# Values by four column tiles, and two mixes side by side, in the first of two window-attention blocks

## The chip, the cores and the metric

The kernel runs on one core of a Trainium2 chip. The metric is the time of one execution on the device in microseconds (us), the median of several. The core's engines are TensorE (PE, with its weight loads shown as PEld), VectorE (DVE), ScalarE (ACT), GpSimd (POOL) and SyncE (SP), which issues the transfers. Each engine works through its own list of instructions in order; semaphores tie the lists together.

## What is computed

Two transformer blocks over 32 images of 56 x 56 tokens with 96 features, float32 in and out. The first has 12 heads and windows of 7 x 7 tokens, shifted by three. The second has 6 heads and windows of 8 x 8. Of the first, cut:

```
xw = windows of roll(x, (-3, -3))                    # 2048 windows of 49 tokens, 96 features
q, k, v = split(xw @ qkv_w + qkv_b)                  # 12 heads of 8 features
attn = cosine(q, k) / max(tau, 0.01) + bias + mask
out = softmax(attn) @ v                              # per window and head
x = x + layernorm(roll back(out @ proj_w + proj_b))
x = x + layernorm(gelu(x @ fc1_w + fc1_b) @ fc2_w + fc2_b)
```

## The kernel before

The first block (`swin_block`) takes its 2048 windows in 256 groups of eight: four pairs of two windows, 392 tokens. The second (`plain_block`) follows when the first is done; the change doesn't touch it.

Each engine has a function `body(g, phase)` that lists its work for one step, written out by hand, and `run_groups` runs it for every group, in a loop over 56 steps written out. The groups are staggered: in step `g`, TensorE turns the input of group `g + 2` and makes its keys, queries and values, scores the pairs of group `g`, turns and mixes the exponentials of group `g - 1`, projects group `g - 2`, and does the MLP of groups `g - 3` and `g - 4`. In a call the first argument is that offset. So `mix(-1, 2)` is the mix of pair 2 of the group before. The order of these calls in `body` is the order in which TensorE works.

TensorE's stages that matter here, with their lines:

- `keys` and `queries` (products at L445 to L447): three products each, stationary 96 x 96, 392 moving columns. `hidden` uses the same lines for its three chunks.
- `turn_probs` (L480): three transposes of a pair's exponentials. ScalarE copies them to `probT` (L623).
- `mix` (L494): exponentials times values for the two windows of a pair. The output's features stand on partitions 0 to 95 in three bands of 32, so each matmul has 32 stationary columns and takes one of three column tiles: 12 matmuls, 24 records, since a float32 matmul shows as two. For pairs 1 and 3 the sums of the exponentials follow (L498), 6 matmuls in the same tiles.
- `values` (L522): for each of eight windows and for the even and the odd heads, one matmul with the window's 49 tokens as stationary columns and 48 moving columns of the weights. Even heads go to PSUM partitions 0 to 48, odd ones to 64 to 112: 16 matmuls, 32 records. ScalarE spreads them to `v_heads` (L663).
- `scores` (L470): stationary 32 x 64, 12 matmuls a pair.
- `key_norms` (L538), `query_norms` (L543): one product each over squared keys and queries.

Three banks of PSUM, A, B and C, serve all dense products by turns. `free(...)` ahead of a stage makes TensorE wait until the bank's last reader is done: the queries' bank by the GELU of the hidden layer's second chunk (`hid`, L700), the query norms' bank by the spreading of the values (`v_heads`, L663). ScalarE does the exponentials, the copies of `probT`, the GELUs with two loads of function tables around them, and several more; VectorE the scores' bias and maxima, the readings of keys and queries and the residuals.

Of the kernel before, what the change touches and what calls it, by code (L numbers as in the profile page):

```python
# [42 lines left out]
HALF = 64  # L43
# [70 lines left out]
def before(group, slot, lag):  # L114

    while slot < lag:
        group, slot = group - 1, slot + PAIRS
    return group, slot - lag


def exists(group, groups):
    return not isinstance(group, int) or 0 <= group < groups
# [14 lines left out]
def swin_block(nc, cfg, src, dst, par, const, psum):  # L137
    win, heads, groups = (cfg.win, cfg.heads, cfg.groups)
    WIN = win * win
    NT = WINDOWS * WIN  # L140
    NTP = NT + 16
    D = DIM // heads
    J = 32 // D
    HP = heads // 2
# [7 lines left out]
    with ctx:  # L152

        def sb(name, shape, dtype=F32):
            return ctx.enter_context(nc.sbuf_tensor(f'{cfg.name}_{name}', shape, dtype))
        did = {name: ctx.enter_context(nc.semaphore(f'{cfg.name}_{name}')) for name in STEPS}

        def upto(group, index=0, per=1):
            return count_for(group, index, per, groups)
        psS = psum['scores']  # L160
        psP = psum['probs']
        psM = psum['dense']
# [30 lines left out]
        xT = sb('xT', [128, 2, NT])  # L193
# [195 lines left out]
        with nc.Block() as block:  # L389
# [47 lines left out]
            def _(pe):  # L437

                def body(g, phase):

                    def parity(d):
                        return (phase + d) % 2
# [6 lines left out]
                    def all_windows(first):  # L449
                        part, pair, column = [list(d) for d in first.ap]  # L450
                        return bass.AP(first.tensor, first.offset, [part, pair, [HALF, 2], column])

                    def free(*uses):
                        for name, d, *place in uses:
                            if exists(g + d, groups):
                                pe.wait_ge(did[name], upto(g + d, *place))
                                break
# [15 lines left out]
                    def turn_probs(d, p, part):  # L473
                        if exists(g + d, groups):
                            pe.wait_ge(did['prob'], upto(g + d, p, PAIRS))
                            ug, us = before(g + d, p, 1)
                            pe.wait_ge(did['probT'], upto(g + d, 2 * p, 2 * PAIRS) if part else upto(ug, 2 * us + 1, 2 * PAIRS))
                            for n in range(3):
                                hp = 3 * part + n
                                last = nc.tensor.transpose(psP[:, n * QT:(n + 1) * QT], prob[0:QT, p, 2 * hp:2 * hp + 2, :].rearrange('p h k -> p (h k)'), ident[0:QT, 0:QT])  # L480
                            last.then_inc(did['prob_turned'], 1)

                    def mix(d, p):
                        if exists(g + d, groups):
                            pe.wait_ge(did['v_heads'], upto(g + d))
                            pe.wait_ge(did['probT'], upto(g + d, 2 * p + 1, 2 * PAIRS))
                            if p % 2 == 0:
                                mg, ms = before(g + d, p, 2)
                                pe.wait_ge(did['mixedT'], upto(mg, ms // 2, 2))
                            for half in range(2):  # L490
                                first = p % 2 * TT + half * WIN
                                for n in range(HB):
                                    for band in range(BANDS):
                                        last = nc.tensor.matmul(psO[32 * band:32 * band + 32, first:first + WIN], v_heads[:, (phase + d) % 4, 2 * p + half, band, n, :], probT[:, p, band * HB + n, half * HALF:half * HALF + WIN], start=n == 0, stop=n == HB - 1)  # L494
                            if p % 2 == 1:
                                for n in range(HB):
                                    for band in range(BANDS):
                                        last = nc.tensor.matmul(psO[32 * band:32 * band + 32, SUMS:SUMS + 2 * TT], sum_heads[:, n, :], all_windows(probT[:, p - 1:p + 1, band * HB + n, 0:WIN]), start=n == 0, stop=n == HB - 1)  # L498
                            last.then_inc(did['mixed_made'], 1)
# [15 lines left out]
                    def values(d, bank):  # L515
                        if exists(g + d, groups):
                            pe.wait_ge(did['xT'], upto(g + d))
                            for w in range(WINDOWS):
                                for odd in range(2):
                                    cols = w_qkv[:, 2 * DIM:3 * DIM].rearrange('c (h o d) -> c h o d', o=2, d=D)[:, :, odd, :]  # L520
                                    out = psM[odd * HALF:odd * HALF + WIN, bank, w * HP * D:(w + 1) * HP * D]
                                    last = nc.tensor.matmul(out, xT[:, parity(d), w * WIN:(w + 1) * WIN], cols, start=True, stop=True)  # L522
                            last.then_inc(did['v_made'], 1)

                    def keys(d, bank):
                        if exists(g + d, groups):
                            pe.wait_ge(did['xT_low'], upto(g + d))
                            product(psM[0:DIM, bank, 0:NT], w_qk_high[:, DIM:2 * DIM], w_qk_low[:, DIM:2 * DIM], xT_high[:, parity(d), :], xT_low[:, parity(d), :]).then_inc(did['k_made'], 1)

                    def queries(d, bank):  # L530
                        if exists(g + d, groups):
                            pe.wait_ge(did['xT_low'], upto(g + d))
                            product(psM[0:DIM, bank, 0:NT], w_qk_high[:, 0:DIM], w_qk_low[:, 0:DIM], xT_high[:, parity(d), :], xT_low[:, parity(d), :]).then_inc(did['q_made'], 1)
# [58 lines left out]
                    turn_probs(-1, 3, 1)  # L592
                    free(('hid', -3, 0, CHUNKS), ('proj_read', -2), ('sq_norm', 1), ('k_read', 1))
                    keys(2, C)
                    mix(-1, 2)
                    free(('hid', -3, 1, CHUNKS), ('x1T_low', -3), ('xT', 2), ('q_read', 1))
                    queries(2, A)
                    turn_probs(0, 0, 0)
                    mix(-1, 3)
                    free(('hid', -3, 2, CHUNKS), ('fc2_read', -4), ('sq_norm', 1), ('v_heads', 1))  # L600
                    values(2, B)
                    scores(0, 3)
                    turn_probs(0, 0, 1)
                    free(('k_read', 2), ('hid', -3, 0, CHUNKS), ('proj_read', -2), ('sq_norm', 1))
                    key_norms(2, C)
                run_groups(pe, groups, 56, body, 16)

            @block.scalar
# [1085 lines left out]
```

## Time and profile before

| | us |
|---|---|
| median of 3 timed runs | 7237.07 (7237.04 to 7237.53) |
| the profiled execution, its time | 7242.55 |
| its span, first to last instruction | 7240.7 |
| TensorE matmuls busy | 6900.7 (95%) |
| TensorE weight loads busy | 5347.6 (74%) |
| ScalarE busy | 6114.9 (84%) |
| VectorE busy | 5941.3 (82%) |
| GpSimd busy | 5286.9 (73%) |

The mean granted clock of TensorE is 0.989 of full speed over the span. The first block takes the first three fifths of it. Busy times are unions: an instruction's time runs from its start until its last result is written, and matmuls follow each other much faster than that, so a stage's cost is read from the starts in a timeline. In a timeline each line merges the neighbouring instructions of one source line: start, time from the first one's start to the last one's end, engine, line, operation, what it writes and reads, shapes (stationary, then moving) and count.

### The profile page before, as it was taken

The page shows a single profiled execution, that of the slowest core. Times are in us where ns is not written, and L with a number is a line of the kernel's source. Part 1 is how long each engine was busy: PE and PEld are TensorE (multiplying, and loading weights), DVE is VectorE, ACT ScalarE, POOL GpSimd, SP SyncE. Part 2 cuts the span into 40 slices and gives each one's busy share as a digit, 9 for nine tenths or more (in the row PEclk, how much of TensorE's full clock was granted, in tenths as well). Part 3 has the DMA queues.
Part 4 walks back from the last instruction along what each step waited for, and adds up shares of the span by engine and source line. Part 5 has one row for each costly group of instructions (what it writes and reads, how often), then busy time and mean ns, then how long its engine had stood idle before and what let it go on. Part 6 is the DMA issues. An engine that isn't in the chain of part 4 may idle for free. (4 is left out here: it accounts for less than half of the span.)

```text
span 7240.7 us, 343768 instructions
## 1 busy us (share of the span) xinstructions
PE 6900.7 (95%) x127358; PEld 5347.6 (74%) x127358; DVE 5941.3 (82%) x12726; ACT 6114.9 (84%) x11052; POOL 5286.9 (73%) x5958
## 2 busy tenths in 40 slices
PE   6999999999999999999999996999999999999998
PEld 4777777777777777777777774777777777777777
DVE  5888888888888888888888884777777777777776
ACT  5999999999999999999999995777777777777777
POOL 3777777777777777777777775777676776776775
PEclk9999999999999999999999997999999999999999
DMA  0111111111111111111111110111111111111111
GB/s 20 30 29 30 29 30 30 29 30 30 30 30 29 30 30 29 30 29 29 30 29 30 29 29 24 42 46 47 45 47 45 45 47 45 47 46 45 46 46 41
DMA packets 367729, 254.62 MB, mean 35 GB/s; under 512 B 271816, under 2 KB 347336, under 8 KB 366152
## 3 DMA queue, kind: packets, MB, share of 16 engines
q1 hardware_dynamic: 366154, 233.04, 12.5%
q8 instruction: 1060, 17.37, 1.0%
q14 instruction: 515, 4.22, 0.2%
HBM read 78.64 MB, written 77.07 MB: 22 GB/s over the span
## 5 line engine op out<-in xcount | busy, mean ns | idle before, releaser
L880 POOL TENSOR_TENSOR swin_score<-swin_score,swin_top 113x588 f32<-113x588 f32 x1024 | 1202.9, 1175 | 744.3 <-DVE swin_top L752 743.8
L623 ACT ACTIVATE swin_probT<-swin_ps_probs 128x339 f32<-128x339 f32 x2048 | 921.8, 450 | 198.5 <-PE swin_ps_probs L480 177.3
L480 PE MATMUL swin_ps_probs<-swin_ident,swin_prob 113*128 113x113 f32 x6144 | 991.1, 270 | 7.0 <-ACT swin_probT L623 7.0
L480 PEld LDWEIGHTS swin_ps_probs<-swin_ident,swin_prob 113*128 113x128 f32 x6144 | 667.4, 141 | 355.3 <-issue 321.5
L747 DVE TENSOR_TENSOR swin_score<-swin_ps_scores,swin_bias_tab 113x588 f32<-113x588 f32 x1024 | 777.1, 759 | 173.7 <-PE swin_ps_scores L470 172.4
L752 DVE TENSOR_REDUCE swin_top<-swin_score 113x12 f32<-113x588 f32 x1024 | 768.8, 751 | 0.2
L1574 POOL TENSOR_TENSOR plain_xT_high<-plain_xT,plain_one 96x512 fp32r<-96x512 f32 x196 | 203.2, 1037 | 719.0 <-ACT plain_xT L1398 719.0
L629 ACT ACTIVATE swin_prob<-swin_score 113x588 f32<-113x588 f32 x1024 | 719.1, 702 | 5.8 <-POOL swin_score L880 2.9
L783 DVE SCALAR_TENSOR_TENSOR swin_x<-swin_y,swin_y_rstd,swin_x_res 98x96 f32<-98x96 f32 x1024 | 601.2, 644 | 0.8 <-POOL swin_y_rstd L898 0.7
L494 PEld LDWEIGHTS swin_ps_mixed<-swin_probT,swin_v_heads 128*32 128x32 f32 x24576 | 422.6, 109 | 223.8 <-issue 145.8
L470 PE MATMUL swin_ps_scores<-swin_k_heads,swin_q_hat 32*64 32x196 f32 (+1 forms) x12288 | 577.7, 347 | 4.8 <-DVE swin_score L747 4.8
L563 PE MATMUL swin_ps_dense<-swin_w_fc,swin_hid 128*98 128x96 f32 x6144 | 575.2, 250 | 1.2 <-ACT swin_hid L700 1.2
L494 PE MATMUL swin_ps_mixed<-swin_probT,swin_v_heads 128*32 128x49 f32 x24576 | 563.3, 210 | 3.2 <-DVE swin_mixedT L760 1.6
L563 PEld LDWEIGHTS swin_ps_dense<-swin_w_fc,swin_hid 128*98 128x98 f32 x6144 | 556.9, 167 | 1.5 <-ACT swin_hid L700 1.5
L1305 PE MATMUL plain_ps_dense<-plain_w_fc,plain_hid 128*64 128x96 f32 x9408 | 439.9, 250 | 73.0 <-ACT plain_v_heads L1390 71.3
L1441 DVE TENSOR_REDUCE plain_top<-plain_ps_scores 128x6 f32<-128x384 f32 x784 | 427.6, 545 | 90.0 <-PE plain_ps_scores L1233 85.8
L1305 PEld LDWEIGHTS plain_ps_dense<-plain_w_fc,plain_hid 128*64 128x64 f32 x9408 | 403.9, 138 | 106.8 <-ACT plain_v_heads L1390 103.1
L886 POOL TENSOR_TENSOR swin_x_res<-swin_x_in,swin_res_row 98x384 f32<-98x384 f32 x256 | 256.2, 1001 | 291.0 <-DVE swin_x L783 235.4
L1262 PEld LDWEIGHTS plain_ps_probs<-plain_ident,plain_prob 128*128 128x128 f32 x2352 | 264.5, 142 | 271.4 <-issue 242.2
L1262 PE MATMUL plain_ps_probs<-plain_ident,plain_prob 128*128 128x128 f32 x2352 | 412.4, 285 | 54.9 <-ACT plain_probT L1363 52.1
L1369 ACT ACTIVATE plain_prob<-plain_score 128x384 f32<-128x384 f32 x784 | 388.9, 519 | 89.0 <-DVE plain_score L1443 83.5
L1375 ACT ACTIVATE plain_hid<-plain_ps_dense,plain_b_fc 128x512 f32<-128x512 f32 x588 | 404.1, 687 | 69.7 <-PE plain_ps_dense L1215 51.1
(191 smaller groups left out, 20635.4 us busy)
## 6 DMA issues: line engine op xcount, KB each, us to landing
swin_k_heads<-swin_k_hat SPq DMA_DIRECT2D x1024, 36.8 KB
plain_x_in<-between_blocks SPq DMA_DIRECT2D x784, 48.0 KB, 2.2
plain_k_heads<-plain_k_hat SPq DMA_DIRECT2D x392, 96.0 KB, 2.5
out_dram<-plain_x SPq DMA_DIRECT2D x784, 48.0 KB
swin_x_in<-in_x SPq DMA_DIRECT2D x224, 136.5 KB
between_blocks<-swin_x SPq DMA_DIRECT2D x224, 136.5 KB
swin_x_in<-in_x SPq DMA_DIRECT2D x224, 19.5 KB
between_blocks<-swin_x SPq DMA_DIRECT2D x224, 19.5 KB
```

Source lines behind the costliest of these rows:

```text
L470: last = nc.tensor.matmul(psS[half * HALF:half * HALF + rows, band, 0:BC], q_hat[part, parity(d), w * WIN:w * WIN + rows], k_heads[part, p ...
L480: last = nc.tensor.transpose(psP[:, n * QT:(n + 1) * QT], prob[0:QT, p, 2 * hp:2 * hp + 2, :].rearrange('p h k -> p (h k)'), ident[0:QT, 0 ...
L494: last = nc.tensor.matmul(psO[32 * band:32 * band + 32, first:first + WIN], v_heads[:, (phase + d) % 4, 2 * p + half, band, n, :], probT[: ...
L563: last = nc.tensor.matmul(psM[0:TT, bank, p * DIM:(p + 1) * DIM], hid[:, c, p * TT:(p + 1) * TT], w_fc2[:, c, :], start=c == 0, stop=c == ...
L623: nc.scalar.activation(to, psP[:, 0:3 * QT], ACT.Copy).then_inc(did['probT'], 1)
L629: nc.scalar.activation(prob[0:QT, p, :, 0:WIN], score[0:QT, p % 2, :].rearrange('p (h k) -> p h k', k=WIN), ACT.Exp).then_inc(did['prob'], 1)
L747: nc.vector.tensor_tensor(score[0:QT, p % 2, :].rearrange('p (b n) -> p b n', b=BANDS), psS[0:QT, :, 0:BC], kind, ALU.add).then_inc(did['s ...
L752: nc.vector.tensor_reduce(top[0:QT, p % 2, :], score[0:QT, p % 2, :].rearrange('p (h k) -> p h k', k=WIN), AX.X, ALU.max).then_inc(did['to ...
L783: last = nc.vector.scalar_tensor_tensor(x1[:, p, :], y[:, p, :], y_rstd[:, p:p + 1], x_res[:, (phase + d) % 4, p, :], ALU.mult, ALU.add)
L880: nc.gpsimd.tensor_tensor(view, view, bcast(top[0:QT, p % 2, :], 2, WIN), ALU.subtract).then_inc(did['shifted'], 1)
L1262: last = nc.tensor.transpose(psP[:, hp * QT:(hp + 1) * QT], prob[0:QT, p, 2 * hp:2 * hp + 2, :].rearrange('p h k -> p (h k)'), ident[0:QT, ...
L1305: last = nc.tensor.matmul(psM[rows:rows + HALF, bank, p * DIM:(p + 1) * DIM], hid[:, c, p * TT + rows:p * TT + rows + HALF], w_fc2[:, c, : ...
```

## The change

In the first block's `values`, each matmul is cut in two along the stationary operand: tokens 0 to 31 and tokens 32 to 48 of the window. The outputs of one window then start on PSUM partitions 0, 32, 64 and 96, which are four column tiles of 32; moving columns, order of windows and results stay. It makes 32 matmuls (64 records) of 16.

In TensorE's list, `mix(-1, 2)` moves from its place between keys and queries to behind `turn_probs(0, 0, 0)`, so that it stands right ahead of `mix(-1, 3)`, and that one right ahead of `values`, as before.

```diff
                             for w in range(WINDOWS):
                                 for odd in range(2):
                                     cols = w_qkv[:, 2 * DIM:3 * DIM].rearrange('c (h o d) -> c h o d', o=2, d=D)[:, :, odd, :]
-                                    out = psM[odd * HALF:odd * HALF + WIN, bank, w * HP * D:(w + 1) * HP * D]
-                                    last = nc.tensor.matmul(out, xT[:, parity(d), w * WIN:(w + 1) * WIN], cols, start=True, stop=True)
+                                    for a, b in ((0, 32), (32, WIN)):
+                                        out = psM[odd * HALF + a:odd * HALF + b, bank, w * HP * D:(w + 1) * HP * D]
+                                        last = nc.tensor.matmul(out, xT[:, parity(d), w * WIN + a:w * WIN + b], cols, start=True, stop=True)
                             last.then_inc(did['v_made'], 1)
...
                     turn_probs(-1, 3, 1)
                     free(('hid', -3, 0, CHUNKS), ('proj_read', -2), ('sq_norm', 1), ('k_read', 1))
                     keys(2, C)
-                    mix(-1, 2)
                     free(('hid', -3, 1, CHUNKS), ('x1T_low', -3), ('xT', 2), ('q_read', 1))
                     queries(2, A)
                     turn_probs(0, 0, 0)
+                    mix(-1, 2)
                     mix(-1, 3)
                     free(('hid', -3, 2, CHUNKS), ('fc2_read', -4), ('sq_norm', 1), ('v_heads', 1))
                     values(2, B)
```

## Rows read from the trace of the kernel before

**Rows 1.** The page's first line.
```profile
span 7240.7 us, 343768 instructions
```

**Rows 2.** Busy time of each engine (instructions), 300 to 4300 us; granted clock, DMA.
```profile
300.00:4300.00 4000.00, 3989.60 (x67137) 3027.99 (x67136) 3561.48 (x5931) 3734.89 (x7118) 3094.56 (x3321) 1.00 0.11 30
```

**Rows 3.** Waits, 300 to 4300 us: who for whom; total us, times, longest.
```profile
ACT swin_probT L623 <- PE swin_ps_probs L480: 159.4, 475, 2.4
...
PE swin_ps_dense L512 <- issue: 8.8, 3, 3.2
...
PE swin_ps_mixed L494 <- DVE swin_mixedT L760: 1.6, 1, 1.6
```

**Rows 4.** TensorE's timeline through one group, 2000 to 2018 us.
```profile
2000.30 0.82 PE L538 MATMUL swin_ps_dense<-swin_qk_sq,swin_same_head 96*96 96x392 f32 x2
...
2001.30 0.82 PE L543 MATMUL swin_ps_dense<-swin_qk_sq,swin_same_head 96*96 96x392 f32 x2
...
2009.09 0.51 PE L480 MATMUL swin_ps_probs<-swin_ident,swin_prob 113*128 113x113 f32 x3
...
2009.81 0.34 PE L447 MATMUL swin_ps_dense<-swin_x1T_high,swin_w_fc_low 96*128 96x392 f32 x1
2009.99 0.34 PE L445 MATMUL swin_ps_dense<-swin_x1T_high,swin_w_fc_high 96*128 96x392 f32 x1
...
2012.04 0.42 PE L445 MATMUL swin_ps_dense<-swin_xT_high,swin_w_qk_high 96*96 96x392 f32 x1
...
2012.75 0.55 PE L494 MATMUL swin_ps_mixed<-swin_probT,swin_v_heads 128*32 128x49 f32 x24
2013.23 0.42 PE L445 MATMUL swin_ps_dense<-swin_xT_high,swin_w_qk_high 96*96 96x392 f32 x1
...
2013.66 0.34 PE L447 MATMUL swin_ps_dense<-swin_xT_high,swin_w_qk_low 96*96 96x392 f32 x1
2013.84 0.45 PE L480 MATMUL swin_ps_probs<-swin_ident,swin_prob 113*128 113x113 f32 x3
2014.23 0.55 PE L494 MATMUL swin_ps_mixed<-swin_probT,swin_v_heads 128*32 128x49 f32 x24
2014.60 0.84 PE L498 MATMUL swin_ps_mixed<-swin_probT,swin_sum_heads 128*32 128x196 f32 x12
2015.38 0.94 PE L522 MATMUL swin_ps_dense<-swin_w_qkv,swin_xT 128*49 128x48 f32 x32
2016.24 0.56 PE L470 MATMUL swin_ps_scores<-swin_k_heads,swin_q_hat 32*64 32x196 f32 x12
...
2017.08 0.82 PE L538 MATMUL swin_ps_dense<-swin_qk_sq,swin_same_head 96*96 96x392 f32 x2
```

**Rows 5.** The same in short windows, which leave the last records of a stage.
```profile
2014.30 0.47 PE L494 MATMUL swin_ps_mixed<-swin_probT,swin_v_heads 128*32 128x49 f32 x20
...
2015.12 0.33 PE L498 MATMUL swin_ps_mixed<-swin_probT,swin_sum_heads 128*32 128x196 f32 x1
...
2015.87 0.45 PE L522 MATMUL swin_ps_dense<-swin_w_qkv,swin_xT 128*49 128x48 f32 x12
...
2016.11 0.21 PE L522 MATMUL swin_ps_dense<-swin_w_qkv,swin_xT 128*49 128x48 f32 x1
```

**Rows 6.** ScalarE's timeline in the same group; in brackets idle time before and releaser.
```profile
2009.64 0.46 ACT L623 ACTIVATE swin_probT<-swin_ps_probs 128x339 f32<-128x339 f32 x1 [0.18 <-PE swin_ps_probs L480]
...
2011.40 1.07 ACT L700 ACTIVATE swin_hid<-swin_ps_dense,swin_b_fc 128x392 f32<-128x392 f32 x2
...
2016.50 0.97 ACT L663 ACTIVATE swin_v_heads<-swin_ps_dense 49x384 f32<-49x384 f32 x2
```

**Rows 7.** TensorE's timeline in the second block, 5500 to 5516 us.
```profile
5503.69 1.03 PE L1245 MATMUL plain_ps_mixed<-plain_v_heads,plain_probT 128*32 128x34 f32 x96
5504.65 1.14 PE L1282 MATMUL plain_ps_dense<-plain_w_qkv,plain_xT 128*64 128x48 f32 x32
```

## The prediction

> **What bounds the kernel now.** I read the page first: one span of 7240.7 us [rows 1]. The kernel runs two blocks one after the other, and the change touches the first alone, so I cut a stretch out of the first block and asked for the busy time of each engine in it [rows 2]. TensorE is busy for 3989.60 of 4000 us at full granted clock (1.00, the 2.4 GHz level). ScalarE has 3734.89, VectorE 3561.48, GpSimd 3094.56. A busy TensorE in this profile is not TensorE at its peak, so the next view is the waits of the same stretch [rows 3]: there TensorE waits four times, some 10 us in all, against 159.4 us that ScalarE's copies of the turned exponentials alone wait for TensorE. So the others wait for TensorE and it waits for nobody: its instruction stream sets the time, and every 0.01 us taken out of a group of eight windows is worth 2.56 us, since the block has 256 groups.
>
> The third view is TensorE's timeline through one group [rows 4]. From one squared-norm product to the same one of the next group it is 16.78 us (2000.30 to 2017.08). In this view I read starts and not durations: an instruction's duration contains its way through the array, and the next one starts long before. What a stage costs is the distance from its start to the next stage's start. The reader is to see that these distances are larger where the shape of the stationary operand changes. One of the six-product runs (keys, queries, hidden layer) goes at 0.18 us a product when the product before it had the same shape: 2009.81 to 2009.99. The first product after a mix takes longer: the queries go from 2013.23 to 2013.66 in two steps, 0.43 us, where two even steps would be 0.36.
>
> **The change, part by part.** All of it is in three pieces, and none adds a DMA or a semaphore.
>
> *A. The mix of pair 2 leaves its place between keys and queries.* Before, keys, mix and queries take 1.80 us, from 2012.04 to the turn at 2013.84 [rows 4]. Without the mix, keys and queries are six products in a row. The first one still follows a turn and costs what it costs the queries now, 0.43 - 0.17 = 0.26 us, and the other five 0.18 us each, the last one's step to the turn included (2013.66 to 2013.84 is 0.18): 1.16 us. That is 0.64 us less. The mix now stands behind the turn and ahead of the other mix. One of the two pays the start behind a turn, as the mix at 2014.23 does today, 0.37 us up to the sums at 2014.60. The other runs on without one. Its price is that of the inner sets: the last 20 matmul records of that mix take from 2014.30 to 2014.60 [rows 5]; three column tiles work side by side, so these are 6.7 sets of three, 0.045 us each by rounded starts. With 0.37 us for all eight sets, start-up included, a set can't be over 0.046; I take 0.044, so 8 x 0.044 = 0.35 us. A = -0.64 + 0.35 = -0.29 us. Bounds: a set at 0.046 and products at 0.185 would give -0.25; a set at 0.040 gives -0.32.
>
> *B. From the sums to the values.* The sums are 12 records in four sets. They start at 2014.60 and the last starts at 2015.12 [rows 5]; with 0.015 us between the tiles of a set that is 0.167 us a set. The values start at 2015.38, 0.78 us behind the first sum, so the fourth set is followed by 0.26 us, not by 0.17. Here the shape goes from 32 columns to 49. With values by 32 columns it stays as it is between mix and sums, where no such gap stands, and I cost it at four sets, 0.67 us. B = -0.11 us. If the gap belongs to the new operands and not to the shape, B is 0.
>
> *C. The values themselves.* Now: 32 records, two tiles side by side, 16 sets, 0.86 us up to the scores at 2016.24. The last six sets go from 2015.87 to 2016.11 [rows 5], five steps and 0.01 us, 0.046 us a set; the whole from 2015.38 to 2016.11 is 15 steps and 0.01, so the first was some 0.03 us longer. From the last record to the scores it is 0.13 us. After: each product becomes two, of 32 and 17 stationary columns, so 64 records and 64 weight loads, four tiles side by side and still 16 sets, because each tile has the same eight windows with the same 48 moving columns in two records each. What is a set worth? The trace has no values by four tiles of this width, so I bound it by rows. The mix moves 49 columns with 32 stationary ones at 0.044; with 48 that is 0.043, which I take, since it is the nearest row in both sizes. Not above 0.046, which 49 stationary columns now need. Four tiles side by side do exist in this trace: the second block's mix, 96 records of 32 stationary and 34 moving columns, from 5503.69 to 5504.65 [rows 7], 0.96 us with its way out, 0.040 us for four. So C is 15 x 0.043 + 0.02 (four tiles start some 0.007 apart) + 0.13 on the way out = 0.80 us against 0.86: C = -0.06 us, with -0.11 (0.040 a set) and 0 (0.046 a set, start-up kept) as ends. The way out keeps its price, as the scores have another shape either way.
>
> **Sum.** -0.29 - 0.11 - 0.06 = -0.46 us. 256 x 0.46 = 118 us. The profiled execution has a span of 7240.7 and a time of 7242.55 us, the median of the timed ones is 7237.07; the saving comes off each of them: 7237 - 118 = 7119 us. The three bounds together give 0.25 to 0.54 us a group.
>
> **What must hold for that.** TensorE is now earlier by 0.46 us in the second half of a group, so its waits there lose as much slack. Three of them matter, all on ScalarE, whose order is fixed. First, the queries wait for the second GELU (their bank). They start at 2012.66 instead of 2013.23; the two GELUs end at 2011.40 + 1.07 = 2012.47 [rows 6], so 0.19 us are left. ScalarE itself is not earlier, its copy at 2009.64 waits for TensorE's turn at 2009.09 in the part that does not change. If the GELU were later, turn, both mixes, values and scores behind the queries in TensorE's queue would all be late with it. Second, the turn of the new group's first pair moves from 2013.84 to 2013.20 and waits for the copy behind the GELUs; that one, 0.46 us long [rows 6], ends at 2012.93 at the latest, so 0.27 us are left. Third, the query norms need the bank that ScalarE frees when it has spread the values: 2016.50 + 0.97 = 2017.47 [rows 6], and they start 1.00 us behind the key norms, at 2018.08; after the change at 2017.62. That leaves 0.15 us, the smallest margin, and it also caps the gain: the loop from TensorE's turn (2009.09) over ScalarE (2017.47) and back over TensorE (1.00 us into a group, to 8.79 us into it) is 8.38 + 7.79 = 16.17 us and a release (that copy starts 0.04 us behind the turn's end, 2009.09 + 0.51), so some 16.22 us, against a new group of 16.32 us. So no sum of terms over about 0.56 us a group could be had: 143 us, 7094 us.
>
> VectorE and GpSimd have idle time of 11% and 23% in the stretch [rows 2], and VectorE gets the queries earlier, which pulls its second half forward as well. The 64 further matmuls and loads a group have to be issued: the second block issues 96 and 96 in 0.96 us [rows 7], 0.010 us for a pair, the values would need 64 pairs in 0.80, 0.0125 us for a pair.
>
> **The rivals.**
> *Slower: every record has its own price.* Now a values record costs 0.023 us (0.73 us for 32). If that is a price by record, and not by columns side by side, 64 of them take 1.47 us, the values grow by 0.75, and the group by 0.75 - 0.29 - 0.11 = 0.35 us: 90 us, 7327 us. It decides from a set of 0.07 us on (the 0.40 us of A and B, on 16 sets). For it: no row shows a 17-column tile, nor four tiles that each move a strided 48 columns. Against it: 0.015 us a record in the mix and 0.010 in the second block's [rows 4, 7], at much the same width. Chance 0.04. A rule that speaks for this rival stands in the Trainium skill, TensorE: Matmul & The Clock Gate, section "Wait — 56ns, not 53.3ns?": however small, matmuls do not start less than about 25 ns apart. By it the values' 64 records would be an estimated 1.6 us, and the kernel some 120 us slower. The trace doesn't agree where tiles differ, with its 0.010 us a record.
> *Part of the gain turns into a wait for ScalarE.* If the release takes longer than the 0.15 to 0.19 us that are left, or ScalarE's chain stretches by 0.2 us when VectorE runs beside it at other times, about 0.2 us come back and 0.26 stay: 67 us, 7170 us. For it: margins under 0.2 us. Against it: ScalarE still waits for TensorE twice a group [rows 3], so it is not the bound. Chance 0.07.
> *No change: the gaps belong to something else* (fetching instructions, say), and appear again at the new neighbours: A stays at the moved mix alone, B and C are 0, within 10 us of 7237. Against it: mix to sums in one shape has no gap, and each change of shape has one. Chance 0.03.
>
> **Numbers.** The forecast has 0.86. 0.2% of the time is 14 us, about what can be told from no change here. Faster 0.93 (the forecast and the partial gain), same 0.03, slower 0.04. The range: from the cap by ScalarE's loop, 7094, to A and C at their low ends with B as it stands, 0.36 us a group, 92 us, 7145. The slower case, the equal one and most of the partial one lie outside, under 2 in 10.
>
> **What would show it.** Right: in the timeline of one group six products in a row at 0.18 us, both mixes together in 0.72 us, 0.67 us from the first sum to the first value, the values with 64 records in 0.80 us to the scores, and 16.32 us from key norms to key norms; TensorE still without waits. Wrong: values over 1.2 us (records have a price), a longer step ahead of the queries or the query norms (ScalarE), or groups of 16.78 us with gaps at new places.

## The result, and the profile after

The changed kernel takes 7171.48 us (four runs, 7164.05 to 7181.03), the one before 7237.3 us: a ratio of 0.9907, 95% interval 0.9891 to 0.9922. It is 66 us faster. The forecast was 118 us, and 7171 lies outside the range that went with it (7094 to 7145).

The profiled execution has a span of 7162.2 us, and in it the usual group is what was forecast (16.30 us against 16.32). TensorE's timeline through one group, with those lines that answer to [rows 4], and then the end of the next group:

```profile
2000.40 0.82 PE L539 MATMUL swin_ps_dense<-swin_qk_sq,swin_same_head 96*96 96x392 f32 x2
...
2012.14 0.42 PE L445 MATMUL swin_ps_dense<-swin_xT_high,swin_w_qk_high 96*96 96x392 f32 x1
...
2012.77 0.34 PE L445 MATMUL swin_ps_dense<-swin_xT_high,swin_w_qk_high 96*96 96x392 f32 x1
...
2013.31 0.46 PE L480 MATMUL swin_ps_probs<-swin_ident,swin_prob 113*128 113x113 f32 x3
2013.69 0.90 PE L494 MATMUL swin_ps_mixed<-swin_probT,swin_v_heads 128*32 128x49 f32 x48
2014.41 0.68 PE L498 MATMUL swin_ps_mixed<-swin_probT,swin_sum_heads 128*32 128x196 f32 x9
2014.77 0.26 PE L523 MATMUL swin_ps_dense<-swin_w_qkv,swin_xT 128*17 128x48 f32 x2
2014.92 0.34 PE L498 MATMUL swin_ps_mixed<-swin_probT,swin_sum_heads 128*32 128x196 f32 x3
2015.08 0.86 PE L523 MATMUL swin_ps_dense<-swin_w_qkv,swin_xT 128*32 128x48 f32 x62
2015.87 0.56 PE L470 MATMUL swin_ps_scores<-swin_k_heads,swin_q_hat 32*64 32x196 f32 x12
...
2016.71 0.82 PE L539 MATMUL swin_ps_dense<-swin_qk_sq,swin_same_head 96*96 96x392 f32 x2
...
2032.17 0.55 PE L470 MATMUL swin_ps_scores<-swin_k_heads,swin_q_hat 32*64 32x196 f32 x4
2032.97 0.55 PE L470 MATMUL swin_ps_scores<-swin_k_heads,swin_q_hat 32*64 32x196 f32 x8 [0.25 <-issue]
2033.45 0.51 PE L480 MATMUL swin_ps_probs<-swin_ident,swin_prob 113*128 113x113 f32 x3
2033.80 0.82 PE L539 MATMUL swin_ps_dense<-swin_qk_sq,swin_same_head 96*96 96x392 f32 x2
```

The first group lasts from 2000.40 to 2016.71, 16.31 us. The next one lasts from 2016.71 to 2033.80, 17.09 us. It has the same instructions; its scores begin at 2032.17 and break off behind four records, and the fifth starts 0.8 us behind the first, "issue" in brackets: the profile shows nothing that TensorE waited for. So one has to look at many groups and not at one. From the starts of the key norms of all 256 groups: the median length is 16.30 us, and 74 of the last 250 groups are over 0.1 us longer than the shortest tenth. Of the kernel before, 3 are, the three at which TensorE's loop returns to its start.

TensorE's waits from 300 to 4200 us, which answer to [rows 3]:

```profile
PE swin_ps_dense L512 <- issue: 17.4, 6, 4.3
PE swin_ps_dense L523 <- issue: 13.3, 22, 1.4
PE swin_ps_scores L470 <- issue: 5.9, 15, 0.8
PE swin_ps_probs L480 <- issue: 3.9, 8, 0.6
```

The last three lines are new, and all four say "issue"; no engine is named. They show less than is lost, since a gap counts only from where the matmuls in flight have ended. From starts alone, each step between two records against the median of that step over all groups, the trace has 82 gaps of over 0.15 us behind the first fifth of a group, 42.6 us in all, in the values, the scores and the turn behind them. The kernel before has none there.

A hint at what TensorE waits for stands in the page's list of transfers. Before:

```profile
q8 instruction: 1060, 17.37, 1.0%
```

After:

```profile
span 7162.2 us, 360152 instructions
...
q8 instruction: 1125, 18.43, 1.1%
```

The change adds 16384 instructions (360152 against 343768 of [rows 1], 64 matmuls and loads in each of 256 groups) and 65 packets on this queue, 1.06 MB, some 65 bytes for each: the queue brings TensorE's instructions. 18.43 MB in 1125 packets are 16 KB each; at 64 bytes an instruction such a packet is a block of 256. The counts fit: 1125 x 256 = 288000, and the trace has 285512 instructions of TensorE, matmuls, loads and those of its sequencer (waits and loop counting). The transfers that begin between 2030.50 and 2032.99 us, the stretch ahead of the gap above:

```profile
q8 instruction: 1, 0.02, 3.1%
```

The same question from 2030.57 on has no such line, so the transfer of a block began within 0.07 us of 2030.50, and TensorE goes on at 2032.97: 2.4 us, of which the transfer itself is some 1.2 us (3.1% of 16 engines' 2.49 us). Below, a block is "asked for" when its transfer begins in the trace. The other gaps are alike: behind the last block asked for, the 82 gaps end after 2.5 us in the median, nine in ten of them after 1.8 to 2.9 us.

That the gaps stand at the ends of blocks can be counted. Number TensorE's recorded instructions in order: between two returns of its loop, and behind the last, the 82 gaps lie whole multiples of 256 instructions apart, to within 16, wherever in a group they fall. The same count gives the place of every block's end, and so how far ahead a block comes. From 300 to 1260 us, a block's transfer begins about when TensorE goes into the block before it, 0.8 us behind that in the median (nine in ten between 0.6 us before and 2.6 us behind). Its first instruction is used 5.4 us after the transfer's beginning in the median and never under 2.2 us. So the next block is under way while one is used up, and no more than that.

### The profile page after: what moved, and what is told of

The parts are those of the page before. It is cut to its first block and busy times, and to the rows that moved or that the text cites. A ratio compares the mean times of both kernels' runs of the same rounds, so it can differ in the third digit from the quotient of the medians.

```text
span 7162.2 us, 360152 instructions
## 1 busy us (share of the span) xinstructions
PE 6791.7 (95%) x135550; PEld 5355.0 (75%) x135550; DVE 6049.8 (84%) x12726; ACT 6094.2 (85%) x11052; POOL 5316.6 (74%) x5958
## 3 DMA queue, kind: packets, MB, share of 16 engines
q8 instruction: 1125, 18.43, 1.1%
## 5 line engine op out<-in xcount | busy, mean ns | idle before, releaser
L881 POOL TENSOR_TENSOR swin_score<-swin_score,swin_top 113x588 f32<-113x588 f32 x1024 | 1206.0, 1178 | 704.0 <-DVE swin_top L753 703.0
L784 DVE SCALAR_TENSOR_TENSOR swin_x<-swin_y,swin_y_rstd,swin_x_res 98x96 f32<-98x96 f32 x1024 | 720.8, 762 | 0.8 <-POOL swin_y_rstd L899 0.7
L494 PEld LDWEIGHTS swin_ps_mixed<-swin_probT,swin_v_heads 128*32 128x32 f32 x24576 | 405.7, 109 | 150.5 <-issue 76.2
L494 PE MATMUL swin_ps_mixed<-swin_probT,swin_v_heads 128*32 128x49 f32 x24576 | 511.2, 209 | 1.9 <-ACT swin_hid L701 1.2
L1444 DVE TENSOR_TENSOR plain_score<-plain_ps_scores,plain_top 128x384 f32<-128x384 f32 x784 | 437.1, 558 | 26.9
```

What stands on the lines that cost most here:

```text
L784: last = nc.vector.scalar_tensor_tensor(x1[:, p, :], y[:, p, :], y_rstd[:, p:p + 1], x_res[:, (phase + d) % 4, p, :], ALU.mult, ALU.add)
L881: nc.gpsimd.tensor_tensor(view, view, bcast(top[0:QT, p % 2, :], 2, WIN), ALU.subtract).then_inc(did['shifted'], 1)
```

## The experiments

Each comparison is with the kernel before on the same chip (7241.93, 7232.49 and 7233.6 us on the three chips), so ratios are to be compared and not times. Two theories went in. S: the instructions come too slowly for the dense stretch, which is 272 loads and matmuls from the moved mix to the end of the scores. R, a rival of the prediction: ScalarE's small margins took part of the gain.

**The order alone.** The values keep their two tiles (edits here are against the changed kernel).

```diff
-                                    for a, b in ((0, 32), (32, WIN)):
-                                        out = psM[odd * HALF + a:odd * HALF + b, bank, w * HP * D:(w + 1) * HP * D]
...
+                                    out = psM[odd * HALF:odd * HALF + WIN, bank, w * HP * D:(w + 1) * HP * D]
```

> The mix moved as in the change, the values as before (two tiles, 32 records). Theory S (supply of instructions: TensorE's come in blocks of 16 KB, 256 instructions, and a block is usable some 2.5 us after it is asked for; a stretch that uses up 256 faster leaves TensorE without any): from the moved mix to the scores there are 208 loads and matmuls in place of 272, in about the same time, so no gaps inside stages; a group takes 16.78 - 0.29 = 16.49 us in every group, 7237 - 74 = 7163 us, and repeated runs agree within a few us. Rival R (ScalarE's margins eat part of the gain): with 0.29 us the smallest margin is still 0.3 us, so 7163 us as well. Rival N (removed gaps turn up at new neighbours): groups of 16.6 us or more.

7170.54 us, ratio 0.9900 (0.9883 to 0.9916), 71 us of the 74. The key norms of three groups in a row, and TensorE's only wait from 300 to 4200 us:

```profile
2000.68 0.82 PE L538 MATMUL swin_ps_dense<-swin_qk_sq,swin_same_head 96*96 96x392 f32 x2
...
2017.17 0.82 PE L538 MATMUL swin_ps_dense<-swin_qk_sq,swin_same_head 96*96 96x392 f32 x2
...
2033.65 0.82 PE L538 MATMUL swin_ps_dense<-swin_qk_sq,swin_same_head 96*96 96x392 f32 x2
```

```profile
PE swin_ps_dense L512 <- issue: 9.8, 3, 3.4
```

16.49 and 16.48 us, and 4 of 250 groups over. Half of the change gives as much as the whole of it. Here the blocks come in time: from 300 to 1260 us the first instruction of a block is used no sooner than 3.4 us after it was asked for.

**The values alone.** The mix of pair 2 goes back between keys and queries, the values keep four tiles.

> The values by four tiles (64 records), the mix of pair 2 left between keys and queries. Theory S: the dense stretch from the mix of pair 3 to the scores has 224 loads and matmuls in some 1.9 us, with six products and a turn ahead of it, so a few blocks come late but fewer than with the change: the usual group takes 16.78 - 0.17 = 16.61 us, and 5 to 25 us are lost to gaps; 7237 - 44 + 15 = 7208 us, range 7195 to 7220. Rival R: nothing is near a limit at a gain of 0.17 us: 7193 us without gaps. If both parts simply added up, this one and the order alone would make the 66 us of the change together.

7214.52 us, ratio 0.9956 (0.9939 to 0.9972), 27 us; S had 29. The usual group is 16.59 us, and 23 of 250 are over. S had the time in part by luck: gaps of over 0.15 us behind the first fifth of a group come to 3.7 us only (S: 5 to 25 us in gaps), and some 12 us more go at the returns of the loop, where the waits went to six with 19.2 us. Added up, the two parts would give 98 us; together they give 66 to 68.

**The scores first.** The scores of pair 3 ahead of the turn behind the queries.

```diff
                     queries(2, A)
+                    scores(0, 3)
                     turn_probs(0, 0, 0)
...
                     values(2, B)
-                    scores(0, 3)
                     turn_probs(0, 0, 1)
```

> The change, with the scores of pair 3 moved from behind the values to ahead of the turn behind the queries: the same instructions, 24 of them out of the dense stretch, and one more change of shape. Theory S: the usual group takes 16.30 + 0.09 = 16.39 us, the gaps become fewer (half or less of what the change loses, 42 us in gaps over 0.15 us): 7165 us, range 7145 to 7180. Rival R: ScalarE's margins are the same or smaller (the values are done 0.5 us later), so the losses stay: 7171 + 23 = 7194 us.

7199.41 us, ratio 0.9941 (0.9925 to 0.9958), 7195 us on the scale of the forecasts. That is what R had (7194), and S missed: it had 7165, at most 7180, and gaps of half or less of 42 us, where 46 gaps with 32.9 us are left. The trace doesn't speak for R, though: the usual group is 16.44 us (S: 16.39), 54 of 250 groups are over (74 with the change), 40 of the 46 gaps stand at ends of blocks by the count above, and the waits from 300 to 4200 us, beside the one at the return of the loop, are "issue" and a little for VectorE:

```profile
PE swin_ps_dense L523 <- issue: 10.9, 19, 0.9
PE swin_ps_probs L480 <- issue: 6.1, 8, 0.9
PE swin_ps_scores L470 <- DVE swin_score L748: 5.3, 6, 1.0
```

24 instructions fewer were no relief: 248 are left, in a stretch that is shorter by the scores' own time. S was right on what is waited for and wrong on how much this order would help.

**Half the records.** Windows 0 to 3 go to PSUM partitions 0 to 48 and windows 4 to 7 to 64 to 112, each with even and odd heads at once: 96 moving columns, the same four tiles, the same columns in all, 32 records. ScalarE spreads them in four copies of half the size.

```diff
...
+                            cols = w_qkv[:, 2 * DIM:3 * DIM].rearrange('c (h o d) -> c o h d', o=2, d=D)
+                            for w in range(PAIRS):
+                                for side in range(2):
+                                    for a, b in ((0, 32), (32, WIN)):
+                                        out = psM[side * HALF + a:side * HALF + b, bank, 0:PAIRS * DIM].rearrange('r (o w c) -> r o w c', o=2, w=PAIRS)[:, :, w]
+                                        first = (side * PAIRS + w) * WIN
+                                        last = nc.tensor.matmul(out, xT[:, parity(d), first + a:first + b], cols, start=True, stop=True)
...
```

> The change, with the values' records halved in the same four tiles: four windows on partitions 0 to 48 and four on 64 to 112, each matmul with all 96 moving columns, 32 records in place of 64; ScalarE spreads them in four instructions of half the size in place of two. Theory S: no gaps inside stages, every group alike; 16.30 us a group if ScalarE's four copies take no longer than 1.0 us together: 7237 - 122 = 7115 us. If they take 0.35 us longer the query norms wait 0.25 us for them: 16.55 us, 7178 us, still without gaps in the values or the scores. Rival R: ScalarE has more to do, so the losses grow: over 7171 us, with TensorE's waits naming ScalarE.

7205.13 us, ratio 0.9943 (0.9926 to 0.996), so by time alone another small gain. The trace tells it apart. TensorE and ScalarE at the end of a group:

```profile
2015.66 0.83 PE L540 MATMUL swin_ps_dense<-swin_qk_sq,swin_same_head 96*96 96x392 f32 x2
2016.32 0.50 PE L512 MATMUL swin_ps_dense<-swin_ident,swin_x_in 98*96 98x98 f32 x4
2016.96 0.90 PE L545 MATMUL swin_ps_dense<-swin_qk_sq,swin_same_head 96*96 96x392 f32 x2
...
2015.59 1.32 ACT L666 ACTIVATE swin_v_heads<-swin_ps_dense 49x192 f32<-49x192 f32 x4
```

and of the waits from 300 to 4200 us, first for TensorE's loads, then for TensorE:

```profile
PEld swin_ps_dense L545 <- ACT swin_v_heads L666: 76.0, 226, 0.3
...
PE swin_ps_dense L512 <- issue: 10.7, 3, 3.6
```

The gaps inside values and scores are gone, 8 of 250 groups are over, and the usual group is 16.65 us. In place of the gaps stands the wait that the prediction had named as the smallest margin: ScalarE's four copies take 1.32 us where the two took 0.97, and the query norms start 1.30 us behind the key norms where 1.00 is the rule. This is what R looks like when it happens, in 226 groups of some 234 and by name. In the changed kernel the query norms start 1.00 us behind the key norms, as before.

**Twice the records.** The change, each product cut at 24 of its 48 moving columns: 128 records.

> The change, with each product of the values cut once more, along its moving columns (24 and 24 in place of 48): 128 records, the same tiles and the same columns in all. Theory S: some 400 loads and matmuls stand between the moved mix and the end of the scores, far over 256, so a block comes late in nearly every group: most groups (over 60%) are over 0.1 us longer than the shortest kind, where the change has 71 of 255, and the time goes over 7230 us. Theory P (only the price of issuing records): the values take 128 x 0.009 = 1.1 us and every group is alike at 16.6 to 16.7 us: 7200 us, or 7170 + 77 = 7248 us with the gaps of the change as they are.

7565.16 us, ratio 1.0459 (1.0438 to 1.048). 183 of 250 groups are over 0.1 us longer than the shortest tenth (16.79 us). TensorE's waits, 300 to 4200 us:

```profile
PE swin_ps_dense L524 <- issue: 135.7, 123, 1.8
PE swin_ps_scores L470 <- issue: 32.2, 26, 1.6
PE swin_ps_dense L512 <- issue: 19.5, 18, 2.6
```

The shortest groups are 0.49 us over those of the change, which is the price of issuing 64 more pairs (0.008 us each); the rest is gaps and what follows from them: the mean granted clock from 300 to 4200 us is 0.98, where the change has 1.00.

**The same number of records, slower.** The order of the change, the values by two tiles of 49 columns, cut at 24 moving columns: 64 records as in the change, but in sets of two tiles in place of four.

> The order of the change, the values by two tiles of 49 columns as before, but each product cut along its moving columns (24 and 24): 64 records as in the change, of which each pair now needs the 0.046 us that 49 columns of weights take to load. The stretch from the moved mix to the scores has the 272 loads and matmuls of the change, in 3.4 us in place of 2.7. Theory S (rate against supply): no gaps inside stages, every group alike at 16.48 + 0.73 = 17.21 us, 7237 + 111 = 7348 us. Theory C (the number of instructions in a group or in the stretch brings the gaps, however fast they are used): uneven groups, about a quarter of them over 0.1 us longer, and 20 us or more above that time.

7354.5 us, ratio 1.0166 (1.0145 to 1.0186), 121 us where S had 111. The usual group is 17.21 us, as S had it. S had no gaps, and there are a few: 25 of 250 groups are over, by 0.6 us at most beside the returns, and of gaps over 0.15 us there are 14 with 4.0 us, where the change has 82 with 42.6. Of TensorE's waits there is left:

```profile
PE swin_ps_dense L512 <- issue: 15.6, 6, 2.9
PE swin_ps_dense L523 <- issue: 0.7, 3, 0.3
```

Same order, same number of instructions, but the dense stretch takes 3.6 us in place of 2.7, and 0.7 us of waits are left in the values against 13.3. It is the rate and not the number.

**Half the records, and the copies shared.** VectorE spreads the last four windows, between its residual and the bias of pair 3.

> As the kernel with halved records, but the values of the last four windows are spread by VectorE (two copies, between its residual and the bias of pair 3), those of the first four by ScalarE (two copies), so that ScalarE has no more to do than before. Theory S, with what the halved records showed (query norms 0.35 us late behind ScalarE's four copies): no gaps inside stages, and no wait at the query norms: 16.30 us in every group, 7237 - 122 = 7115 us (7105 to 7135), under the change and under the order alone. If VectorE's copies come too late for the query norms, up to 0.2 us a group of it is lost: 7165 us. If the gaps of the change were a matter of four tiles and not of instructions, they would be here too: 7165 us or more, with uneven groups.

7308.19 us, ratio 1.0103 (1.0086 to 1.012). The groups are even (3 of 250 over), but 17.10 us long. TensorE and VectorE:

```profile
2011.69 0.83 PE L543 MATMUL swin_ps_dense<-swin_qk_sq,swin_same_head 96*96 96x392 f32 x2
...
2013.48 0.87 PE L548 MATMUL swin_ps_dense<-swin_qk_sq,swin_same_head 96*96 96x392 f32 x2 [0.61 <-issue]
...
2009.73 2.88 DVE L787 SCALAR_TENSOR_TENSOR swin_x<-swin_y,swin_y_rstd,swin_x_res 98x96 f32<-98x96 f32 x4
2012.64 0.73 DVE L854 COPY swin_v_heads<-swin_ps_dense 49x192 f32<-49x192 f32 x2
```

VectorE's residual takes 2.88 us until 2012.61, its copies end at 2013.37, and the query norms wait for them until 2013.48, 0.8 us. (The profile says "issue" here; in TensorE's list the wait for these copies stands at this place.) My edit had put them behind the wrong instruction.

**Half the records, the copies earlier.** ScalarE spreads all the values, and its logarithm of the sums comes behind and not ahead of that.

```diff
-                    log_totals(-1, 1)
                     spread_values(2, B)
+                    log_totals(-1, 1)
                     copy_turned(0, 0, 1)
```

> The kernel with halved records, with ScalarE's logarithm of the sums (0.21 us) moved from ahead of the four copies of the values to behind them. Theory S: as no block of instructions comes late with halved records, the wait of the query norms for ScalarE is all that is left, and it shrinks by 0.21 us, from 0.35 to 0.14: 16.44 us in every group, 7237 - 86 = 7151 us (7140 to 7165), under the change and under the order alone by 15 us.

7152.47 us, ratio 0.9885 (0.9869 to 0.9902), 81 us. The usual group is 16.46 us, and 15 of 250 are over, by 0.2 us at most beside the returns. The profile lists no wait of TensorE's matmuls but that at the return of its loop (it leaves out what is under 0.15 us). What is left of the limit is ScalarE: the query norms start 1.10 us behind the key norms, 0.06 us behind the end of the copies (2015.89), and last 0.90 us where 0.82 is the rule, which together is the 0.16 us over the changed kernel's usual group:

```profile
2014.85 0.83 PE L540 MATMUL swin_ps_dense<-swin_qk_sq,swin_same_head 96*96 96x392 f32 x2
2015.95 0.90 PE L545 MATMUL swin_ps_dense<-swin_qk_sq,swin_same_head 96*96 96x392 f32 x2
...
2014.57 1.32 ACT L666 ACTIVATE swin_v_heads<-swin_ps_dense 49x192 f32<-49x192 f32 x4
...
2031.31 0.83 PE L540 MATMUL swin_ps_dense<-swin_qk_sq,swin_same_head 96*96 96x392 f32 x2
```

This has the lowest ratio of the study, though its group is longer by 0.16 us than the changed kernel's usual one. Its interval and that of the changed kernel, run again on another chip, overlap a little, so that it is the faster of the two is likely and not shown.

**The changed kernel again.**

> The changed kernel once more, on the chip of these runs, to compare with: 7165 to 7185 us. By theory S its runs differ among themselves by more than those of the kernel with halved records, since it depends on when blocks of instructions arrive.

7164.62 us, ratio 0.9903 (0.9886 to 0.9919), on a chip on which the kernel before took 7232.49. Its four runs lie 13 us apart (7154.78 to 7167.66), those of the last version 8 (7149.73 to 7157.63); with runs of the kernel before up to 14 us apart that proves nothing on the spread. The usual group is 16.30 us and 70 of 250 are over, as in the first profile.

## Why the prediction was wrong

**What bounds the kernel: right for the first block.** TensorE's stream set the time there, and still does outside the gaps. "It waits for nobody" was read from the first block alone; in the second, from 4500 to 7200 us, the kernel before has these waits of TensorE:

```profile
PE plain_ps_dense L1282 <- issue: 34.0, 31, 1.6
PE plain_ps_dense L1290 <- issue: 17.9, 23, 1.4
```

**A, B and C: right, to a few hundredths.** Keys and queries to the turn: 2012.14 to 2013.31, 1.17 us (forecast 1.16). Both mixes up to the sums: 0.72 (0.72). The first sum to the first full set of values: 2014.41 to 2015.08, 0.67 (0.67). Values to scores: 0.79 (0.80). The usual group is 16.30 us (16.32), so that 255 groups of it would have given 122 us.

**The step that failed is the last sentence ahead of the rivals**, that the 64 further matmuls and loads "have to be issued", priced at nothing since the second block issues a pair in 0.010 us. That row shows that TensorE can take 192 instructions at such a rate when it has them. It doesn't show that they arrive at that rate. ("None adds a DMA" was wrong in the same way: the 64 more instructions a group come in 65 more packets over the run.) The two halves of the change add their instructions to one stretch: 96 of the mixes, 24 of the sums, 128 of the values, 24 of the scores, from 2013.69 to 2016.36, where the kernel before has 160 from 2014.23 on. More than a block of 256 in 2.7 us, with some 2.5 us from the asking for a block to its use: when the end of a block falls badly, TensorE runs dry. The block's end moves through the group, as a group's 668 instructions are no multiple of 256, and so it happens in some three groups of ten and at different places. The second block's 288 from 5503.69 on take 3.2 us, until the wait at 5506.89, and that group doesn't show the limit. Others of the same block do. The two waits above are at the values (L1282), right behind the mix that [rows 7] show, and at the projection behind them; with the rest, and without the four at the returns of its loop, the second block of the kernel before has 57 waits put down to "issue", 53.6 us, and by the count of instructions 56 of them stand at ends of blocks, to within two instructions. So the price that the prediction left out was in the trace that it was read from, some groups beside the row.

The Trainium skill has the block, in Advanced Engine Details and Errata, section "ISA Cache": a cache line holds 16 KB, 256 instructions. The trace agrees with the 256 (16 KB a packet, 64 bytes an instruction). The section also says that there are only two lines, and gives TensorE 128 KB, which would be an estimated eight; the trace goes by two, as a block is asked for about when the one before it is begun, and some 150 to 240 instructions were executed between asking and going on.

**The account.** 122 us of shorter groups; less 46 us for gaps inside groups, of which 42.6 are the 82 gaps over 0.15 us; less 8 us at the three returns of TensorE's loop, where the wait at the head of the loop went from three times and 8.8 us [rows 3] to six times and 17.4 us. That leaves the 68 us by which the first block is shorter from its first to its last key norms (4284.7 to 4216.4 us).

**The rival that fitted by number fitted by accident.** "Part of the gain turns into a wait for ScalarE" had 7170 us. With half the records, where that wait did occur, it stood in nearly every group and at the query norms. In the changed kernel no wait of TensorE's matmuls names ScalarE from 300 to 4200 us. One of its weight loads does, 179 times, at the turn behind the query norms; but that turn starts 0.66 us behind the query norms with the change (first three lines) as before it (the last, with 2001.30 of [rows 4]), so it cost nothing:

```profile
PEld swin_ps_probs L480 <- ACT swin_probT L624: 40.0, 179, 0.2
2001.40 0.82 PE L544 MATMUL swin_ps_dense<-swin_qk_sq,swin_same_head 96*96 96x392 f32 x2
2002.06 0.46 PE L480 MATMUL swin_ps_probs<-swin_ident,swin_prob 113*128 113x113 f32 x3
...
2001.96 0.45 PE L480 MATMUL swin_ps_probs<-swin_ident,swin_prob 113*128 113x113 f32 x3
```

The prediction's "fetching instructions, say" stood in the rival of no change, as an idea of why the gaps at changes of shape were there; they were of the shape, as forecast, and the fetching came on top.

**What is shown and what isn't.** Shown is that records over time cause the gaps: four tiles with half the records have none, with twice the records most groups have them, and the same 64 records in a dense stretch of 3.6 us have few. Shown by the count of instructions is that the gaps stand at the ends of blocks. What else is in the 2.5 us beside the transfer was not measured. The return of the loop costs 2.7 us more with 64 records a group, in every kernel that has them (19.2 us in six waits with the values alone, 10.7 in three with half the records). There the trace of the changed kernel shows a second wait: after the block with the loop's head has come, TensorE goes on for nine instructions and waits 2.4 us for the next. So the loop's head lies close to the end of a block. That it does so by the number of instructions ahead of the loop fits; no run moved it by itself.

## What to carry to other kernels

When a change packs small matmuls more tightly, count the instructions in the densest few microseconds, loads included, and set them against the blocks in which the queue of instructions brings them and against the time from a block's request to its use; a row that shows a fast burst of 192 says nothing about 272. Look for waits put down to "issue" in the whole trace, also in parts that the change doesn't touch: here the second block had the limit on show. Look at the lengths of many groups and not at one, since such gaps fall on some groups only and the median group hides them. And look for the same work in fewer, longer records: here 96 moving columns in place of 48 gave the four tiles without the gaps, and moved the limit to ScalarE's copies.

## What the runs showed of the hardware that was not expected

Where TensorE stood waiting for it, a block of 256 instructions was usable 1.8 to 2.9 us after its transfer began (nine gaps in ten), with this kernel's other transfers beside it. A matmul need not wait for those ahead of it in the list when its column tile is free: the first records of the fourth tile start at 2014.77, ahead of the last set of sums at 2014.92, which precede them in the program. And VectorE's residual, four instructions, takes 2.36 us in the usual group of the kernel before and 2.88 us with the change. Three of the four take 0.30 us and one takes the rest: it ends 0.12 us behind GpSimd's L880 (L881 with the change), at 2016.93 behind 2016.81 before and at 1968.02 behind 1967.90 after. In the last experiment the four take 0.99 us, and it is GpSimd's instruction beside them that takes 1.87 us in place of 1.17. That one of the two engines holds up the other fits all three; no run was made to try it.
